# Reordering VectorE's gates and gated lo part around the K block transposition, and moving one TensorE transposition by a chunk

## What is computed

```python
h = tok(log_dt, Lambda, x)                        # K = Re(sum over n of Wc[c,h,n] * exp(dt_Lambda[h,n] * l)), l < 1024
h = h + layernorm(h) @ (weight * block_mask).T    # 1024 x 1024, "attention"
y = layernorm(h)
logits = y @ W_router.T + b_router                # 8 experts
weights = sparsemax(logits)                       # the "gates"
h = h + y @ W_base.T + b_base + sum_e weights[e] * (y @ lora_A[e]) @ lora_B[e]
```

## Time and profile before

| | us |
|---|---|
| median of 3 runs | 535.89 (535.52 to 536.78) |
| the profiled execution's own time | 535.71 |
| its span in the profile | 533.9 |
| TensorE busy (matmuls) | 486.2, 91% of the span |
| VectorE busy | 411.5, 77% |
| ScalarE busy | 255.9, 48% |
| GpSimd busy | 125.7, 24% |

### The profile page before, as it was taken

One profiled execution on the slowest core, in us unless ns is written; L12 is line 12 of the kernel. 1 busy time (PEld: TensorE's weight loads), 2 busy tenths in 40 slices (PEclk: granted clock), 3 DMA queues, 4 the chain that ended last, 5 costly groups with the idle time before them and its releaser, 6 DMA issues.

```text
span 533.9 us, 7434 instructions
## 1 busy us (share of the span) xinstructions
PE 486.2 (91%) x2467; PEld 407.1 (76%) x2467; DVE 411.5 (77%) x866; ACT 255.9 (48%) x469; POOL 125.7 (24%) x110
## 2 busy tenths in 40 slices
PE   3257978889899999999999999999999999999995
PEld 2155757778687888888887888787888888888884
DVE  7989866898787987888787878788988878764241
ACT  3763385947263554646463626263644546323200
POOL 0577952630020303030303020020303030303020
PEclk9996989989999999999999999999999999999999
DMA  8994013021212121221203031212121211212011
GB/s 298 400 294 101 1 46 118 1 83 45 79 47 79 44 79 44 61 62 39 83 19 88 17 88 35 79 44 79 44 79 46 79 41 41 79 35 84 1 39 39
DMA packets 28763, 40.82 MB, mean 76 GB/s; under 512 B 10760, under 2 KB 21192, under 8 KB 28744
## 3 DMA queue, kind: packets, MB, share of 16 engines
q1 hardware_dynamic: 28368, 40.49, 25.1%
q10 hardware_dynamic: 376, 0.10, 0.1%
HBM read 23.80 MB, written 16.78 MB: 76 GB/s over the span
## 4 chain that ended last, share of the span: by engine, by line
PE 36%; DVE 35%; issue 17%; ACT 9%; POOL 1%; DVEq 1%; DMA 0%; ACTq 0%; POOLq 0%
PE acc_b L455 15%; PE acc_a L455 13%; DVE b_sb L1127 4%; PE turnp L448 2%; DVE tmp L1093 2%; DVE tmp L1112 2%; PE turnp L439 2%; DVE x_lo L1174 2%; ACT x_hi L715 2%; ACT x_hi L680 2%; DVE b_sb L1111 2%; PE small L479 1%; DVE st L1135 1%; PE acc_b L420 1%; DVE wa_raw L1015 1%
## 5 line engine op out<-in xcount | busy, mean ns | idle before, releaser
L917 POOL TENSOR_TENSOR h<-h,st 128x1024 f32<-128x1024 f32 x16 | 30.3, 1894 | 337.7 <-PE turnp L448 337.7
L455 PE MATMUL acc_a<-wa_hi,x_hi 128*128 128x512 f32 x256 | 84.1, 405 | 0.5 <-DVE h L1145 0.5
L455 PE MATMUL acc_b<-wb_hi,x_hi 128*128 128x512 f32 x256 | 84.5, 406 | 0.0
L455 PE MATMUL acc_a<-wa_lo,x_hi 128*128 128x512 f32 x256 | 81.6, 395 | 0.0
L455 PE MATMUL acc_b<-wb_lo,x_hi 128*128 128x512 f32 x256 | 81.3, 394 | 0.0
L455 PE MATMUL acc_a<-wa_hi,x_lo 128*128 128x512 f32 x256 | 81.2, 393 | 0.0
L455 PE MATMUL acc_b<-wb_hi,x_lo 128*128 128x512 f32 x256 | 80.9, 392 | 0.0
L455 PEld LDWEIGHTS acc_a<-wa_hi,x_lo 128*128 128x128 f32 x256 | 48.8, 190 | 10.6
L455 PEld LDWEIGHTS acc_b<-wb_hi,x_lo 128*128 128x128 f32 x256 | 48.5, 189 | 10.6
L455 PEld LDWEIGHTS acc_b<-wb_lo,x_hi 128*128 128x128 f32 x256 | 48.5, 189 | 10.5
L455 PEld LDWEIGHTS acc_a<-wa_lo,x_hi 128*128 128x128 f32 x256 | 48.8, 191 | 10.1
(11 more groups left out here) (201 smaller groups left out, 913.9 us busy)
## 6 DMA issues: line engine op xcount, KB each, us to landing
h<-rows_out SPq DMA_DIRECT2D x16, 512.0 KB, 3.2
out<-h SPq DMA_DIRECT2D x15, 512.0 KB
rows_out<-b_sb SPq DMA_DIRECT2D x56, 128.0 KB, 2.3
mask_raw<-in_L_attn_mask SPq DMA_DIRECT2D x8, 512.0 KB, 9.8
wa_raw<-in_L_attn_weight SPq DMA_DIRECT2D x8, 512.0 KB, 10.5
wb_raw<-in_L_ffn_W_base SPq DMA_DIRECT2D x8, 512.0 KB, 14.7
rows_out<-tmp SPq DMA_DIRECT2D x8, 128.0 KB, 2.3
xn<-in_x SPq DMA_DIRECT2D x15, 64.0 KB
```

What stands on the lines that cost most here:

```text
L455: return pe.matmul(cols, a, rows, start=first, stop=last)
L917: pool.tensor_tensor(h2[par][:, :], h2[par][:, :], st2[:, par, 1:2].to_broadcast([P, L]), ALU.subtract)\
```

## The change

In VectorE's step, `gates(t-1)` goes ahead of `k_turn(t+1)`, and `gated_low(t-1)` goes ahead of `table_v(t+2)`, between it and `v_factors(t+2)`. In TensorE's step, `gated_transpose(t-1)` stands ahead of chunk 5 of `base` and no more ahead of chunk 6. No operation is added or taken away, and no semaphore or buffer changes. The prologue and the code behind the steps stay as they are.

```diff
@@ TensorE, step @@
                         x_transposes(t + 2)
                     if k == KC // 2 and at(t, TILES - 1):
                         h2_transposes(t, par)
-                    if k == KC - 2:
+                    if k == KC - 3:
                         gated_transpose(t - 1)
                     base(t - 1, k)
@@ VectorE, step @@
                 attention_residual(t, par)
                 if real(t + 1):
                     k_low(t + 1)
+                gates(t - 1, 1 - par)
+                if real(t + 1):
                     k_turn(t + 1)
-                gates(t - 1, 1 - par)
                 if real(t + 2):
                     v_factors(t + 2)
+                gated_low(t - 1)
+                if real(t + 2):
                     table_v(t + 2)
-                gated_low(t - 1)
                 if at(t, TILES - 1):
                     h2_low(t)
```

## The result

The changed kernel took 530.88 us (median of 5 runs, 529.23 to 531.08), the kernel before beside it 536.52 us (5 runs, 535.52 to 536.78). The ratio is 0.9892, with a 95% interval of 0.9876 to 0.9909: **faster by 1.1%**. Forecast were 528.9 us, in a range of 527.9 to 531.6.

A forecast was written before the change was run, and what follows sets the result against it. The prediction took TensorE's waits for VectorE's hw_lo, once a step, as the bound. Gains of 2.41 us in step 2 and 4.54 in steps 3 to 13 made 6.95, giving 528.9 us after 0.18 us to the median; range 527.9 to 531.6.

The forecast's parts named there:

- What bounds the kernel: Steps 2 to 13: TensorE's weight load for the experts waits for VectorE's hw_lo, 8.2 us in 12 steps.
- The gates, and the turn 2.78 us later: VectorE's step: hw_sb done at about 250.3, the K block's turn 2.78 us later, at no cost.
- The slack of 5.6 us: ScalarE: h1 may land 5.6 us later, 1.3 before its sum and 4.3 of waiting before its exponentials.
- The transposition: TensorE's gated_transpose one chunk, 1.37 us, sooner: 254.40 to 253.03, no wait for hw_sb, no added cost.
- gated_low ahead of table_v: VectorE: new wait of 0.02 to 0.1 us, table_v ends 0.37 later, hw_lo 3 us before TensorE wants it.
- What is late next: Steady steps: nothing else holds TensorE; VectorE has 1.25 us of slack before the result, table_b 2.0 us.
- The sum: Whole kernel: step 2 gains 2.41 us, steps 3 to 13 gain 4.54, the rest nothing; together 6.95 us.
- the step put together from two parts: TensorE's step without a wait: 23.90 us to the gates' transposition plus 4.21 to the next begin, 28.11 us.
- GpSimd in step 2: Step 2: VectorE's L1095 ends at about 143.5, GpSimd begins at about 143.6; cost taken as 0, bound 0 to 1 us.
- Only the steady steps gain: Rival: after step 2 VectorE lacks slack, so its 2.41 us return as a later wait; 531.3 us, chance 0.09.
- The wait is only moved: Rival: VectorE's loop is longer than read, the stall reappears at h2_low or the K block; 535.9 us, chance 0.05.
- The K rows land too late: Rival: the later turn's landing holds up ScalarE's sum, 1.0 us in each of 13 steps; 542 us, chance 0.03.

The follow-up runs named there:

- the three reductions: The changed kernel with three more VectorE reductions a step in table_v, from tile 4 on, results unused: 530.11 us in one execution, steps of 28.21 us.

## Why the prediction was right

**What bounds the kernel**: right. The loop over VectorE was there, and hw_lo was its only hold on TensorE in the steps. The move of the gated lo part alone took it away.

**The gates, and the turn 2.78 us later**: right. SyncE's first DMA of step 6 stands 249.05 - 227.13 = 21.92 us behind the step's beginning, where the earlier trace rows make 19.20, 2.72 later. ScalarE's sum shows no wait in steps 4 to 13, and 0.43 us in step 3. The slack of 5.6 us was right in size, but the limit that was seen is not the one that was named. In the changed kernel h1 lands at about 252.66 + 3.2 = 255.9, and `table_b`'s L1111, which waits for the same landing, begins at 261.45: 5.6 us too. The path over the exponentials, 1.5 us before the sum and 4.3 behind it, has nearly the same length, and no run tells the two apart.

**The transposition**: right. It stands 22.56 us behind the step's beginning; 22.5 was forecast. But its move and the gates' were named as parts of the gain, and they carry none. The prediction costed the three parts together and never asked what each brings alone. Its own rows had the answer: with hw_hi at 254.99 and 1.75 us of VectorE's waiting, gated_low could wait 1.4 us for it.

**gated_low ahead of table_v**: right. L1181 begins 0.62 behind L487, and L1092 begins 23.38 behind the step's beginning, where it was 253.60 - 230.50 = 23.10: 0.28 later, and 0.37 was forecast.

**What is late next**: right that nothing is, too low in size. VectorE's spare time was put at 1.25 us before the result, and it was 3.3 in the step, as the three reductions showed. 1.27 of it hid in an operation's duration: in the kernel before, too, L1139 took 1.42 us at 263.04, beside GpSimd's addition. "In the steady steps they do not meet" holds for the operations that were moved, and not for this one.

**The sum**: 6.95 us were forecast, the two profiled executions differ by 6.48. Step 2 gave 2.36 (forecast 2.41), steps 3 to 13 gave 4.28 (4.54): the step put together from two parts, 28.11, came out at 28.13, which is 0.3 us over eleven steps. The rest is the prologue's 0.19. The medians differ by 5.64 only, and the median is 2.0 over the forecast. It also lies outside of the prediction's own range for the full gain, 527.9 to 530.0. What kept it within the stated range was the room up to 531.6, given for the sake of a rival that did not come true. So the mechanism was right, and the hit of the number is in part luck.

The profiled executions flatter both kernels: that of before is 0.8 under the median of its five runs, 536.52, and that of the changed kernel, 529.23, is the fastest of its five, 1.65 under theirs. The forecast took the first for typical, and it had no term for the prologue, whose length differed by 1.7 us between two executions of the changed kernel. That is nearly the size of the error.

**GpSimd in step 2**: the near miss came, by 0.6 us where 0.1 was forecast. In the changed kernel L1095 ends at 142.01 + 1.22 = 143.23, and GpSimd begins at 143.85. The Trainium skill's rule ("SBUF — State Buffer", section "Who interferes with whom"), that a VectorE instruction with two SBUF inputs and a GpSimd instruction that reads SBUF exclude each other for the whole length of the first, agrees with the rows here: 3.20 us for L1096 is 2.1 until GpSimd's L920 ends at 115.88, and 1.1 behind it, where the operation takes 1.22 undisturbed. An instruction with one input in PSUM is not held: in the changed kernel L1187 takes 1.27 us at 118.58, all of it beside L920. So "the engines meet only through semaphores", as the description of the chip has it, is not all: VectorE stands still for GpSimd here with no semaphore between them.

**The rivals.** "Only the steady steps gain" falls with step 2's 28.16. "The wait is only moved" falls with the chain of waits. "The K rows land too late" falls with the kernel that writes them twice.

## What to carry to other kernels

When two engines hand work to and fro and both have idle time, look for the small operation that one of them is ready for and hasn't reached, and put it ahead of the large ones; a wait in front of it costs nothing up to the idle time that this engine has elsewhere in the loop. A wait for an answer to its own earlier work, as VectorE's 1.70 us for ScalarE's x_hi, is no such idle time. Before moving several things together, ask of each whether it is late by itself: here one of three was. And count as idle time also what an operation is longer than its kind, for that is a wait which the table of waits doesn't list.

## What was not expected of the hardware

- A VectorE operation on one column per partition took 1.43 us beside GpSimd's L920 and 0.16 without it, one of 64 columns 2.13 and 0.21.
- Behind a wait of 2.14 us TensorE's granted clock fell from 1.00 to 0.64 over the next 4.3 us; with a wait of 0.17 us at the same place it stayed at 1.00. Behind the 3.19 us in the prologue it was 0.58 over 4 us. In step 2 of the kernel before it stayed at 1.00 behind a wait of 1.96 us. TensorE's row and the stretch behind that wait:

```profile
143.40 0.73 PE L455 MATMUL acc_b<-lb_hi,hw_hi 128*128 128x512 f32 x2 [1.96 <-DVE hw_lo L1181]
...
143.30:147.30 4.00, 3.90 (x21) 3.34 (x22) 1.54 (x3) 1.27 (x2) 1.29 (x1) 1.00 0.00 0
```

- Two executions of the same program differed by 1.7 us, nearly all of it ahead of tile 0's h2 transposes at 83 us. At most 0.6 of it, in a stretch with a granted clock of 0.92 or 0.84, is shown to go with the clock. Each of the steps behind it took the same time within 0.02 us.
